# A graph layer on one core: neighbour rows fetched by three engines, rows in four pieces, more of them on SyncE and ScalarE

## The reference

```python
h = jnp.maximum(_layernorm(x, axis=-1), 0.0)
agg = jax.ops.segment_sum(h[src], dst, num_segments=N)   # 200000 rows of h are fetched and added
z = (1.0 + eps_gin) * h + agg
t = jnp.dot(z, W1) + b1                                  # 256 -> 512
t = jax.nn.relu(_batchnorm(t, g1, bt1))                  # mean and variance over all nodes
conv_out = jnp.dot(t, W2) + b2                           # 512 -> 256
out = jax.nn.relu(_batchnorm(conv_out + h, g2, bt2))
return x + out
```

## Time and profile before

| | us |
|---|---|
| median of 3 runs | 2143.66 (2143.52 to 2145.73) |
| the profiled execution, as timed | 2143.43 |
| its span | 2141.6 |
| GpSimd busy in it | 1449.2 (68%), 1540 instructions |
| TensorE busy | 1430.6 (67%) |
| VectorE busy | 768.3 (36%) |
| ScalarE busy | 338.3 (16%) |
| mean granted TensorE clock | 0.831 |

### The profile page before, as it was taken

One profiled execution on the slowest core, in us unless ns is written; L12 is line 12 of the kernel. 1 busy time (PEld: TensorE's weight loads), 2 busy tenths in 40 slices (PEclk: granted clock), 3 DMA queues, 4 the chain that ended last, 5 costly groups with the idle time before them and its releaser, 6 DMA issues.

```text
span 2141.6 us, 24025 instructions
## 1 busy us (share of the span) xinstructions
PE 1430.6 (67%) x4835; PEld 911.2 (43%) x4835; DVE 768.3 (36%) x1947; ACT 338.3 (16%) x661; POOL 1449.2 (68%) x1540
## 2 busy tenths in 40 slices
PE   3656666665655766675666566666666666689998
PEld 2434344443433434343444334434344444454446
DVE  7777753222322222322232222222232232234447
ACT  6767660000000000000000000000000000014446
POOL 7777777777777777777777777777777777760000
PEclk7788788877888787888888887778787788899999
DMA  6666654444434434444444443443443444448438
GB/s 200 214 224 218 225 175 129 132 117 139 138 108 139 138 110 136 137 118 130 136 126 119 138 139 108 138 137 107 140 137 108 136 135 123 137 133 321 176 135 319
DMA packets 123554, 325.22 MB, mean 152 GB/s; under 512 B 32179, under 2 KB 55294, under 8 KB 117266
## 3 DMA queue, kind: packets, MB, share of 16 engines
q0 software_dynamic: 73440, 200.64, 32.0%
q1 hardware_dynamic: 39100, 97.34, 12.8%
q10 hardware_dynamic: 10870, 25.75, 3.6%
HBM read 271.55 MB, written 52.05 MB: 151 GB/s over the span
## 4 chain that ended last, share of the span: by engine, by line
POOL 65%; issue 21%; PE 12%; DMA 2%; ACT 0%; DVE 0%; SPq 0%; POOLq 0%; DVEq 0%
POOL arena L650 65%; PE ps L1442 8%; PE ps L1324 2%; PE ps L1456 2%; DMA arena<-h_rows,arena 1%; PE ps L1360 0%; PE ps L1398 0%; DMA arena<-in_src 0%; ACT aggT L1072 0%; SPq L439 0%; ACT arena L1078 0%; ACT arena L1076 0%; DVE arena L1057 0%; PE ps L1334 0%; SPq L433 0%
## 5 line engine op out<-in xcount | busy, mean ns | idle before, releaser
L650 POOL DMA_INDIRECT arena<-h_rows,arena x1292 | 1221.6, 946 | 394.0 <-issue 391.5
L1324 PE MATMUL ps<-arena 128*96 128x256 f32 x3060 | 976.9, 489 | 675.2 <-DMA arena<-h_rows,arena 561.5
L1324 PEld LDWEIGHTS ps<-arena 128*96 128x96 f32 x3060 | 640.8, 216 | 993.3 <-issue 732.4
L840 DVE TENSOR_TENSOR aggT<-aggT,ps 128x192 f32 x196 | 69.3, 353 | 1074.2 <-PE ps L1334 1071.2
L1151 ACT COPY arena<-ps 96x256 f32<-96x256 f32 x37 | 13.2, 357 | 1575.5 <-PE ps L1334 1545.0
L650 POOL DMA_INDIRECT arena<-in_x,arena x222 | 209.9, 946 | 67.7 <-issue 67.7
L1360 PE MATMUL ps<-arena 128*128 128x512 f32 (+3 forms) x412 | 186.3, 577 | 1.6 <-DVE arena L873 1.5
L1442 PE MATMUL ps<-arena,W2s 128*128 128x512 f32 (+1 forms) x400 | 168.1, 582 | 0.9 <-ACT arena L1272 0.8
L927 DVE TENSOR_TENSOR arena<-arena,ps 128x768 f32<-128x768 f32 x159 | 149.8, 942 | 0.0
L1103 ACT ACTIVATE arena<-arena,nb,mv 128x256 f32<-128x256 f32 x238 | 120.2, 587 | 83.6 <-DVE nb L744 81.5
L1442 PEld LDWEIGHTS ps<-arena,W2s 128*128 128x128 f32 x400 | 75.7, 190 | 93.2 <-issue 86.3
(11 more groups left out here) (99 smaller groups left out, 575.2 us busy)
## 6 DMA issues: line engine op xcount, KB each, us to landing
W2s<-h_rows ACTq DMA_DIRECT2D x2176, 1.0 KB
rl_odd<-h_rows SPq DMA_DIRECT2D x1792, 1.0 KB
t_T<-arena SPq DMA_DIRECT2D x24, 1024.0 KB, 4.9
arena<-t_T SPq DMA_DIRECT2D x24, 1024.0 KB, 4.8
arena<-h_rows,arena POOLq DMA_INDIRECT x1292, 2.8
arena<-in_x SPq DMA_DIRECT2D x27, 512.0 KB, 5.7
h_rows<-arena ACTq DMA_DIRECT2D x24, 512.0 KB, 3.4
out<-arena SPq DMA_DIRECT2D x23, 512.0 KB
```

The source lines that it names most:

```text
L650: nc.gpsimd.indirect_dma_start(out=rows[slot(g)][:, k, :], out_offset=None, in_=(x if g < H_FROM else h_dram)[:, :], in_offset=bass.Indire ...
L840: V.tensor_tensor(z, z, winT_ps, ALU.add).then_inc(s_add, 1)
L1324: last = T.matmul(win_ps[g % 2], sel[:, g % 2, k, :], rows_of(g, k), start=k == 0, stop=k == n - 1)
```

## The change

Four things.

- `SP_EIGHTHS` goes from 12 to 22 (44 rows a pass) and `ACT_EIGHTHS` from 7 to 11 (22 rows a group). `sp_groups` becomes 10, 16, 22, 28 (x part) and 38, 44, 50, 56, ... 190 (27 groups of the h part): 31 tiles. `act_groups` becomes 38, 44, 50, ... 190: 27 tiles. GpSimd fetches the rest, 1505 tiles instead of 1530.
- A row of the h part is written as four runs of 256 bytes, with 16 bytes between two of them in the buffer (`PART_PITCH = 68` floats), and read from DRAM as four runs of 256 bytes side by side. It stays one DMA. TensorE reads such a tile with a two-level pattern. Rows of `x` are still written whole.
- `t` is stored in two halves of 512 KB instead of once 1 MB, the first half in pass 8+4q (waits for two of the chunk's four blocks), the second in pass 9+4q. The waits on `s_td` count 32 instead of 16 a chunk.
- The strips of offsets move to other memory; SyncE's first `load_at` therefore waits for `s_flag` as well.

The core of the diff:

```diff
-SP_EIGHTHS = 12
-ACT_EIGHTHS = 7
+SP_EIGHTHS = 22
+ACT_EIGHTHS = 11
+HALF_T = FB // 2
+ROW_PARTS = 4
+PART_PITCH = 68
+ROW_PITCH = ROW_PARTS * PART_PITCH
...
-        sp_rows = [rl_odd[:, b * D:(b + 1) * D] for b in range(ROW_BUFS)]
-        sp_at = [rl_odd[0:1, ROW_BUFS * D + b * P:ROW_BUFS * D + (b + 1) * P].bitcast(i32) for b in (0, 1)]
+        sp_bufs = [rl_odd[:, b * ROW_PITCH:(b + 1) * ROW_PITCH] for b in range(ROW_BUFS)]
+        sp_at = [early_[0:1, n:n + P].bitcast(i32) for n in (FB * NQ * 6, FB * NQ * 6 + P)]
...
+        def in_parts(buf):
+            return buf.rearrange("p (b e) -> p b e", e=PART_PITCH)[:, :, 0:D // ROW_PARTS]
...
+            def store_half_t(q, half):
+                a, b = half * HALF_T, (half + 1) * HALF_T
+                sp.wait_ge(s_tb, FB * q + b)
+                sp.dma_start(t_dram[q, :, a:b, :], tb[:, a:b, :]).then_inc(s_td, 16)
...
-                    a = x_bytes if j < SP_X else h_bytes
-                    sp.dma_start(sp_rows[j % ROW_BUFS][e:e + 1, :].bitcast(mybir.dt.uint8),
-                                 a[bass.ds(at, ROW_BYTES)].rearrange("(p e) -> p e", p=1)
-                                 ).then_inc(s_sprows[j % ROW_BUFS], 16)
+                    buf = sp_bufs[j % ROW_BUFS].bitcast(mybir.dt.uint8)[e:e + 1, :]
+                    if j < SP_X:
+                        sp.dma_start(buf[:, 0:ROW_BYTES], x_bytes[bass.ds(at, ROW_BYTES)].rearrange("(p e) -> p e", p=1)
+                                     ).then_inc(s_sprows[j % ROW_BUFS], 16)
+                    else:
+                        sp.dma_start(buf.rearrange("p (b e) -> p b e", b=ROW_PARTS)[:, :, 0:ROW_BYTES // ROW_PARTS],
+                                     h_bytes[bass.ds(at, ROW_BYTES)].rearrange("(p b e) -> p b e", p=1, b=ROW_PARTS)
+                                     ).then_inc(s_sprows[j % ROW_BUFS], 16)
...
-                if 2 * Q < c < NT - 1 and c % Q == 1:
-                    q = (c - 2 * Q - 1) // Q
-                    if q == NQF - 3:
-                        sp.wait_ge(s_td, 16 * q)
+                if 2 * Q <= c < NT - 1 and c % Q <= 1:
+                    q, half = divmod(c - 2 * Q, Q)
+                    if q == NQF - 3 and half == 0:
+                        sp.wait_ge(s_td, 32 * q)
                         load_t(0, 0, 0)
-                    store_t(q)
+                    if q <= NQF - 3:
+                        store_half_t(q, half)
...
                     sp.wait_ge(s_atd, 16)
+                    sp.wait_ge(s_flag, 1)
                     load_at(0)
...
-                    act.dma_start(act_rows[j % ROW_BUFS][e:e + 1, :].bitcast(mybir.dt.uint8),
-                                  h_bytes[bass.ds(at, ROW_BYTES)].rearrange("(p e) -> p e", p=1)
+                    buf = act_bufs[j % ROW_BUFS].bitcast(mybir.dt.uint8)[e:e + 1, :]
+                    act.dma_start(buf.rearrange("p (b e) -> p b e", b=ROW_PARTS)[:, :, 0:ROW_BYTES // ROW_PARTS],
+                                  h_bytes[bass.ds(at, ROW_BYTES)].rearrange("(p b e) -> p b e", p=1, b=ROW_PARTS)
                                   ).then_inc(s_actrows[j % ROW_BUFS], 16)
...
-                    last = T.matmul(win_ps[g % 2], sel[:, g % 2, k, :], rows_of(g, k),
-                                    start=k == 0, stop=k == n - 1)
+                    win = win_ps[g % 2]
+                    if g >= H_FROM and (sp_tile(g, k) or act_tile(g, k)):
+                        win = win.rearrange("p (b e) -> p b e", b=ROW_PARTS)
+                    last = T.matmul(win, sel[:, g % 2, k, :], rows_of(g, k), start=k == 0, stop=k == n - 1)
```

More of the change, by code:

```diff
@@ L216, in build @@
         rl_odd = rl[1].rearrange("p f n -> p (f n)")
-        sp_rows = [rl_odd[:, b * D:(b + 1) * D] for b in range(ROW_BUFS)]
-        sp_at = [rl_odd[0:1, ROW_BUFS * D + b * P:ROW_BUFS * D + (b + 1) * P].bitcast(i32) for b in (0, 1)]
+        sp_bufs = [rl_odd[:, b * ROW_PITCH:(b + 1) * ROW_PITCH] for b in range(ROW_BUFS)]
+        sp_at = [early_[0:1, n:n + P].bitcast(i32) for n in (FB * NQ * 6, FB * NQ * 6 + P)]
+        assert FB * NQ * 6 + 2 * P <= n_early
         w2_early = W2s.rearrange("p f d -> p (f d)")
-        act_rows = [w2_early[:, b * D:(b + 1) * D] for b in range(ROW_BUFS)]
-        act_at = [w2_early[0:1, ROW_BUFS * D + b * P:ROW_BUFS * D + (b + 1) * P].bitcast(i32) for b in (0, 1)]
+        act_bufs = [w2_early[:, b * ROW_PITCH:(b + 1) * ROW_PITCH] for b in range(ROW_BUFS)]
+        act_at = [w2_early[0:1, ROW_BUFS * ROW_PITCH:ROW_BUFS * ROW_PITCH + P].bitcast(i32),
+                  rl_odd[0:1, ROW_BUFS * ROW_PITCH:ROW_BUFS * ROW_PITCH + P].bitcast(i32)]
+        assert ROW_BUFS * ROW_PITCH + P <= FB * D
         mv1 = sb("mv1", [P, FB, 2])
@@ L319, in slot @@
             return 4 if g % RG == 1 and g >= H_FROM else g % RG
+        def in_parts(buf):
+            return buf.rearrange("p (b e) -> p b e", e=PART_PITCH)[:, :, 0:D // ROW_PARTS]
         def rows_of(g, k):
             if sp_tile(g, k):
-                return sp_rows[sp_groups.index(g) % ROW_BUFS]
+                buf = sp_bufs[sp_groups.index(g) % ROW_BUFS]
+                return buf[:, 0:D] if g < H_FROM else in_parts(buf)
             if act_tile(g, k):
-                return act_rows[act_groups.index(g) % ROW_BUFS]
+                return in_parts(act_bufs[act_groups.index(g) % ROW_BUFS])
             return rows[slot(g)][:, k, :]
@@ L475, in store_t @@
                 if q < NQF:
-                    sp.dma_start(t_dram[q, :, :, :], tb[:, :, :]).then_inc(s_td if q < NQF - 1 else s_td_full, 16)
+                    sp.dma_start(t_dram[q, :, :, :], tb[:, :, :]).then_inc(s_td_full, 16)
                 else:
@@ L537, in _ @@
                 if c == NT - 1:
-                    store_t(NQF - 2)
+                    for half in (0, 1):
+                        store_half_t(NQF - 2, half)
                 if c < H_NODES:
@@ L573, in _ @@
             store_t(NQF)
-            sp.wait_ge(s_td, 16 * (NQF - 1))
+            sp.wait_ge(s_td, 32 * (NQF - 1))
             sp.wait_ge(s_bn1, 1)
@@ L922, in h_step @@
                     if m == 0:
-                        dve.wait_ge(s_td, 16 * q)
+                        dve.wait_ge(s_td, 32 * q)
                     V.tensor_scalar(tb[:, m, :], t_ps[(FB * q + m) % TB][:, 0:QN], b1T[:, m:m + 1], None, ALU.add
@@ L1156, in t_and_b1 @@
                     if m == 0:
-                        act.wait_ge(s_td, 16 * q)
+                        act.wait_ge(s_td, 32 * q)
                     act.wait_ge(s_tst, FB * (q - 1) + m + 1)
```

## The result

| | before | after |
|---|---|---|
| median | 2143.69 us (2143.52 to 2145.73, 4 runs) | 3540.36 us (3526.33 to 3544.93, 4 runs) |
| ratio, 95% interval | | 1.650 (1.645 to 1.655) |
| the profiled execution, its span | 2143.4, 2141.6 | 3540.7, 3538.9 |
| GpSimd's gathers from `h_rows` | 1292 | 1269 |
| GpSimd's waits for TensorE | 2.4 us | 1415.9 us |

The change makes the kernel 1.65 times as slow. The prediction had 2113 us with a range of 2109 to 2152, and its dearest rival stood at 2181: the result is 1359 us beyond that.

The account below looks back on a forecast made before the run. GpSimd's gathers were taken as the bound, at 1.251 us each: 25 fewer save 31.3 us, so 2143.4 becomes 2112.1, and 1 us lost where the h part begins makes 2113 us, range 2109 to 2152.

Parts of the forecast that it names:

- dearest rival, (1): Rows of the h part: four pieces cost 43 ns more a row, time 2181 us; slower, mostly this, chance 0.23.
- p: Extra issue time of an h-part row in four pieces, in ns: taken as 15, between 0 and 43.
- differences of 43 ns: Three traced DMAs of four 512-byte runs: the later two cost 43 ns more, read as price or as waiting.
- the prediction's own formula: ScalarE's last h-part tile is ready at 376 + 26 x 54.0 + 3.456 p, in time up to 1860.
- SyncE's rate: SyncE's four passes in the h part: 74.1 us with rows in pieces, against 76.6 us for eight groups.
- two lots of 23.36 us: SyncE's tile: 64 rows and a register load took 23.36 us; a whole tile was put at some 49.6 us.
- SyncE would not bind first: In the h part SyncE passes its limit at p = 30, later than ScalarE at p = 23.
- ScalarE's 54.0 us a tile: ScalarE's h-part tiles not held back by a buffer start 54.0 us apart; one is due every 56.0 us.
- the tail of some 225 us: After the last gather TensorE's work, 217.5 of 224.6 us, stays unchanged.
- The hand-over: Where the h part begins: window 29's copy moves to about 341, leaving 5 to 7 us of slack; 1 us added.
- Rival (3): Transfers bind: single rows crowd few DMA engines, gathers land late, time near 2143 us; within 0.2%, with this, chance 0.05.

Follow-up runs that it names:

- m1: Program of its own without the graph layer, 32 DMAs of 1 KB per form: one run 0.22 us, two to sixteen runs 0.54 to 0.62.
- e10: Kernel after with rows whole again, 31 and 27 tiles, where the kernel before takes 2148.9 us: 2154.2 us, ratio 1.0017.
- m2: Second program without the layer, more DMA forms, both engines issuing, rows beside gathers or a copy: 128 whole rows beside gathers took 106.4 us.
- f3: Kernel after with the old numbers (12 and 7), rows still in four pieces, beside a kernel before of 2145.0 us: 2396.4 us, ratio 1.117.
- f1: Kernel after with whole rows, SP_EIGHTHS = 20 and ACT_EIGHTHS = 11, beside a kernel before of 2145.0 us: 2117.8 us, ratio 0.987.
- f2: Kernel after with whole rows, SP_EIGHTHS = 18 and ACT_EIGHTHS = 10, beside a kernel before of 2145.0 us: 2123.7 us, ratio 0.990.
- e5: Kernel after with whole rows and the old numbers (16 and 17 tiles): 2570.8 us against 2577.6 for the kernel before, ratio 0.999.
- e1: Kernel after with rows whole again, 31 and 27 tiles, where the kernel before takes 2569.3 us: 3151.5 us, ratio 1.227.

## Why the prediction failed, step by step

**The step that failed is p**, the extra issue time of a row in four pieces: 15 ns taken, 0 to 139 given as its bounds; it is 403 ns on ScalarE (638 less 235) and 372 on SyncE (600 less 228). Both ends were read from rows of the cheap form. So the costly term was mis-sized, 15 ns for some 400, and with it the path: SyncE and ScalarE, not GpSimd, set the pace. The earlier trace rows are DMAs of four partitions with one run each; m1 has that form at 255 and 295 ns and the change's at 577. The earlier trace rows are 128 partitions, one run each; an operation that is large isn't an upper bound for one that is of another kind, and this one is cheaper, 328 against 577 ns. The rows' differences of 43 ns, over which the prediction argued at length, had nothing to do with the question. The text itself said that no row of the trace shows a one-partition DMA in four runs; that sentence should have widened the range to "a form not priced here, so without a bound above", and its rivals with it. And the trace did hold one DMA with gapped runs, the store L478 above: 0.643 us against 0.361 for the same store without gaps, 282 ns more. As an upper bound for p it would have been nearer than 139 and still too low.

**The rest of the sum, with p measured, gives the result.** ScalarE's last tile by the prediction's own formula, 376 + 26 x 54.0 + 3.456 x 403, is ready at 3173; its last row was issued at 3187.7. SyncE, which the prediction thought to have more in hand (p = 30 against 23), is later: last row at 3278.1, and from there to the end of the span at 3538.9 are 260.8. A tile of SyncE took (3278.1 - 296.4) / 27 = 110.4 us. The working, with the slip of the next point put right, gives 51.7 + 0.128 x 372 = 99.3, and 2.4 for loads of `h` and stores of `t`. Where the other 8.7 us are shows when the trace's durations are added up and held against e10, the same program with whole rows. A tile is 51.7 us longer (110.4 against 58.7): 37.0 of it in the row DMAs, 4.1 in the MOVEs and 9.8 in the gaps around the two. The gaps and the MOVEs have the form of the hold-up that the m2 program showed on B. Why rows in pieces bring it to A stays open. With old numbers, f3, the same sum holds: ScalarE's 17 tiles take (2121.9 - 317.4) / 17 = 106.1 us each, and from the last row 270 us follow to the end of the span at 2391.9.

**SyncE's rate was too good even without pieces.** The prediction had 74.1 us for four passes, less 2.6 at p = 0, against 76.6 allowed. e10 shows tiles 58.7 us apart, that is 80.7 for four passes. One register load of 2.1 us a tile was left out by a slip: two lots of 23.36 us hold one load each, so a tile has two more, and takes 51.7, not 49.6 us. The larger part is that SyncE's issues lengthen: 25% of them took over 0.26 us in e10, against 6% before, with the same median of 0.228, at most 3.95 us; the mean is 0.264 us against 0.232, which is 4.1 us a tile. One tile's rows with the three register loads among them took 50.91 us there; by the earlier trace rows they are 2 x 23.36 + 2.1 = 48.8. Of 58.7 us 51.7 and 2.4 are accounted for, and these 4.1 are nearly all of the other 4.6. With 20 and 11 in f1, 21% are long still, with a mean of 0.246; only 18 and 10 in f2 is back at 6%. ScalarE's go the same way: 7% over 0.26 us before and in f2, 21% in f1, 25% in e10. What in the fuller program stretches them wasn't found. GpSimd then waits 43.7 us. On the chip of e10, 2148.9 - 31.3 + 43.7 = 2161 is the sum, and e10 took 2154.2; the sign fits, some 7 us don't.

**That SyncE would not bind first** was therefore wrong: at 22 it binds by itself, at 20 it doesn't (177.1 us to spare). The working had 2.5 of 76.6 us in hand, less than one of its terms was uncertain by.

**Right were:** that GpSimd bounds the kernel and 1.25 us fall away with each gather (f1 and f2: 1.30 and 1.33 a gather); ScalarE's 54.0 us a tile (e10: 54.9; the parts that the prediction names for it, 128 x 0.325 and four loads of 2.2, make 50.4, but it is the measured 54.0 that went into the sum); the tail of some 225 us; that the halves of `t`, the moved strips and the wait for `s_flag` cost nothing that can be measured (e5, ratio 0.999, on B; on A, f1 and f2 gain what their gathers give, with all three in them); and that TensorE reads a tile in pieces for nothing. The matmuls of SyncE's tiles in the kernel after (count, busy, mean ns):

```profile
L1352 PE MATMUL ps<-rl_odd,arena 128*96 128x256 f32 x62 | 18.4, 379 | 0.0
```

They take 379 ns as in f1, where the rows are whole, and as in the kernel before (379); eight of the 62 are tiles of `x`, whose rows are whole. The hand-over was thin as told: with rows in pieces GpSimd's first two waits there are 14.5 and 4.2 us, at 353 and 378 us.

**Of the rivals**, (1) had the right mechanism: the issue of a row gets dearer, GpSimd waits for TensorE, TensorE for rows, and this to the last group. It was sized at p = 43, about a ninth of what it was. Rival (3), that transfers bind, is out: the DMA engines' share fell to 0.24 in the h part. The small packets did grow, by the page 83756 under 512 bytes against 35372 in e10, that is 48384 = 6912 rows x 7, with 6912 x 6 more packets in all: eight small ones where a large and a small one were. Nothing shows that they cost time beside the issue. The m1 program has 256-byte runs in a cheap form, four partitions at 0.255 us, but with nothing beside them; no run of the layer has small packets without the dear form, so this isn't separated.

**The rule of the Trainium skill** (page "DMA: Bandwidth & Descriptors", section "Issuing engines are not separate DMA queues", that the sequencer's time is usually small relative to the DMA) isn't borne out by this kernel: a sequencer is busy for 0.6 us with 1 KB, and the kernel's time is that, at a DMA share of 0.24. The prediction put the rule aside for the right reason and then took its price from the wrong row.

## What to carry to other kernels

Price a DMA issue by a row of the same form of pattern (whether a second level remains in it after runs that touch are merged) before you count bytes or partitions; a row of another form is neither its price nor its bound. Where an engine's issue time is within a few per cent of what is asked of it, take care with the number of items too: with whole rows 20 instead of 22 turned +5 us into -27. And when the edit's form isn't in the trace, leave the range open on that side.

## What was not expected of the hardware

- A one-KB DMA costs its engine 0.21 to 0.24 us if its pattern merges to one run, and 0.54 to 0.63 us with a second level inside, whether two runs or sixteen, on the DRAM side or in the buffer, from a register or fixed; four partitions of one run each take 0.255 to 0.295. A DMA of 128 partitions with 1 KB each takes 0.33, or 0.54 with four runs in each. Two DMAs of the kernel before with 128 partitions and four runs take 0.406 (L467) and 0.643 (L478).
- SyncE and ScalarE issuing the dear form together take 0.64 us each instead of 0.58; with whole rows 0.228 and 0.231, against 0.207 to 0.221 and 0.213 alone.
- The issues of whole rows stretch as the program fills: of SyncE's 25% take over 0.26 us at 44 rows a pass (e10), 21% at 40 (f1), 6% at 36 (f2) and at 24 (before).
- The same kernel has a median of 2144 to 2149 us in some comparisons and 2569 to 2578 in others, and each tile fetched by rows makes it worse in the second sort (2471 with three such tiles, 2571 with 33, 2816 with 45, 3152 with 58). Shown is that single instructions of SyncE, MOVEs too, take up to 0.74 us while GpSimd gathers, with gaps as long between them. Loads of code aren't visibly slower there: the packets of the profile's instruction queue 14 have a median of 0.40 us in e1 on B and in f1 on A alike. Whether the sort is of the chip, and what makes it, stays open.
